# Head norm and output gate moved from the batch and the projection to the quarter that reads them, in a fused RWKV and cross-attention kernel

## What is computed

```python
xa = _ln(x, ln1_w, ln1_b)
sx = jnp.concatenate([state[:, 1:2] - xa[:, :1], xa[:, :-1] - xa[:, 1:]], axis=1)
xxx = jnp.tanh((xa + sx * maa_x) @ maa_w1).reshape(b, l, 5, DM)
xxx = jnp.einsum('blfd,fde->blfe', xxx, maa_w2)
xm = xa[:, :, None] + sx[:, :, None] * (maa_stack + xxx)      # five mixes
w = jnp.exp(-jnp.exp(time_decay + jnp.tanh(xw @ td_w1) @ td_w2))
r, k, v = xr @ Wr.T, xk @ Wk.T, xv @ Wv.T
g = jax.nn.silu(xg @ Wg.T)
def step(s, rkvw):                                            # 128 steps, per head
    a = k_t[..., :, None] * v_t[..., None, :]
    out = jnp.einsum('bhi,bhij->bhj', r_t, u * a + s)
    s = a + w_t[..., :, None] * s
    return (s, out)
og = ((og - m) / jnp.sqrt(va + 1e-05)).reshape(b, l, e) * gn_w + gn_b   # norm by head
x1 = x + og * g @ Wo.T
...                                                           # second layernorm and shift: xk2, xr2
y = x1 + sigmoid(xr2 @ Wfr.T) * (square(relu(xk2 @ Wfk.T)) @ Wfv.T)
# then per batch: instance norms, 1x1 convolutions, softmax attention of y over ctx, 1x1 convolution, + y
```

## Time and profile before

| | us |
|---|---|
| median of three runs | 1023.35 (1020.78 to 1023.88) |
| the profiled execution | 1016.36 |
| its span from first to last instruction | 1014.6 |
| PE busy | 896.1 (88%) |
| DVE busy | 691.5 (68%) |
| POOL busy | 536.5 (53%) |
| ACT busy | 396.5 (39%) |
| mean granted TensorE clock | 0.936 of 2.4 GHz |

### The profile page before, as it was taken

How to read it: one execution, slowest core, us unless ns; L and a number is a source line. 1 busy time by engine, 2 the same in 40 slices (tenths; PEclk the granted TensorE clock), 3 DMA queues, 4 the chain that set the end, 5 groups by cost and what they waited for, 6 DMA issues and landing times.

```text
span 1014.6 us, 10745 instructions
## 1 busy us (share of the span) xinstructions
PE 896.1 (88%) x3588; PEld 398.5 (39%) x3588; DVE 691.5 (68%) x907; ACT 396.5 (39%) x819; POOL 536.5 (53%) x573
## 2 busy tenths in 40 slices
PE   1679978799786899688998999899998999979998
PEld 1233433343322343243343444344443454444454
DVE  6234499789988687888887698988998224442342
ACT  2013412333212241133223254565355554465395
POOL 2000388669987749648886778889682101000010
PEclk9687997899977899698999999999999999999999
DMA  7351679969689877878979844779642022001001
GB/s 270 134 125 73 179 178 222 233 171 233 162 187 216 209 184 196 212 145 224 243 182 281 216 112 100 183 192 227 163 99 83 21 73 83 21 4 39 21 0 42
DMA packets 100089, 150.69 MB, mean 149 GB/s; under 512 B 22850, under 2 KB 64066, under 8 KB 91842
## 3 DMA queue, kind: packets, MB, share of 16 engines
q1 hardware_dynamic: 73410, 129.03, 50.4%
q10 hardware_dynamic: 26624, 20.98, 8.5%
HBM read 115.38 MB, written 33.55 MB: 147 GB/s over the span
## 4 chain that ended last, share of the span: by engine, by line
PE 59%; DVE 14%; POOL 12%; issue 6%; ACT 5%; ACTq 2%; DMA 2%; SPq 0%; POOLq 0%; DVEq 0%
PE PS L1318 38%; PE PS L1381 4%; PE PS L1543 4%; POOL VB L704 4%; PE PS L1440 3%; PE PS L1520 2%; DVE PS L1033 2%; PE PS L1325 2%; POOL VB L699 2%; DVE VB L1150 2%; DVE M L1030 2%; DVE VB L1030 2%; POOL VB L695 2%; DVE M L1033 2%; PE PS L1454 1%
## 5 line engine op out<-in xcount | busy, mean ns | idle before, releaser
L1318 PE MATMUL PS<-M,W 128*128 128x512 f32 x672 | 329.8, 634 | 23.7 <-DVE M L1033 12.3
L1318 PEld LDWEIGHTS PS<-M,W 128*128 128x128 f32 x672 | 128.7, 202 | 198.2 <-issue 167.5
L704 POOL TENSOR_TENSOR VB<-VB 128x1024 f32<-128x1024 f32 x64 | 151.4, 2366 | 58.9 <-ACT VB L849 56.2
L1150 DVE TENSOR_TENSOR_SCAN VB<-PS,VB 128x512 f32<-128x512 f32 x128 | 149.1, 1206 | 25.9 <-POOL VB L704 17.3
L587 POOL TENSOR_SCALAR NM<-MV 128x2 f32<-128x2 f32 (+1 forms) x24 | 6.2, 258 | 283.7 <-DVE MV L1278 183.0
L1030 DVE TENSOR_TENSOR VB<-VB,PS 128x2048 f32<-128x2048 f32 x64 | 145.9, 2280 | 1.5
L695 POOL TENSOR_TENSOR VB<-KR,VB 128x1008 f32<-128x1008 f32 x64 | 129.7, 2026 | 17.5 <-DMA VB<-scr_vs 17.5
L699 POOL TENSOR_TENSOR VB<-WG,VB 128x1008 f32<-128x1008 f32 x64 | 129.3, 2020 | 0.0
L1033 DVE SCALAR_TENSOR_TENSOR PS<-PS,VEC,SX 128x512 f32<-128x512 f32 x80 | 60.2, 752 | 87.7 <-PE PS L1381 72.4
L1318 PE MATMUL PS<-W,M 128*128 128x512 f32 x224 | 105.1, 595 | 0.0
L1296 DVE TENSOR_REDUCE SM<-PS 128x1 f32<-128x512 f32 x64 | 44.0, 688 | 58.9 <-PE PS L1543 58.4
(11 more groups left out here) (167 smaller groups left out, 1280.5 us busy)
## 6 DMA issues: line engine op xcount, KB each, us to landing
VB<-scr_vs SPq DMA_DIRECT2D x64, 1024.0 KB, 7.9
W<-in_w SPq DMA_DIRECT2D x8, 1024.0 KB, 9.8
X<-in_x SPq DMA_DIRECT2D x4, 1024.0 KB, 8.2
scr_vs<-STG ACTq DMA_DIRECT2D x64, 64.0 KB, 5.7
scr_v<-STG ACTq DMA_DIRECT2D x16, 256.0 KB, 6.9
scr_w<-STG ACTq DMA_DIRECT2D x16, 256.0 KB, 8.3
scr_k<-STG ACTq DMA_DIRECT2D x16, 256.0 KB, 2.7
KR<-scr_k SPq DMA_DIRECT2D x16, 256.0 KB, 8.1
```

What stands on the lines that cost most here:

```text
L704: po.tensor_tensor(flat(bv[:, 0]), flat(bv[:, 0]), flat(bv[:, 1]), ALU.add).then_inc(g_kv, 1)
L1150: sc = dv.tensor_tensor_scan(s_, PS[:, 5, :], b_, 0.0, ALU.mult, ALU.add)
L1318: mm = pe.matmul(o, l, r, start=i == 0, stop=i == 3)
```

## The change

1. **Norm by quarter.** After OT is assembled it is stored at once: `end` loses ACT's square and copy, PE's two small products, POOL's Newton steps and DVE's last multiplication. In c, `norm_gate` (ACT) squares the loaded quarter, 4 x 512 columns; PE takes the variance of a quarter with 16 matmuls of 128 columns; POOL runs Newton on 128 columns (`stream_n`) and writes a masked 128x512 operand; PE spreads it with one matmul of 512 columns; DVE (`normed`) does twelve `scalar_tensor_tensor`: times gn_w and the root, (tanh + 1) times g, plus gn_b times that.
2. **Gate by quarter.** ACT stores g/2 (`ACT.Copy`, scale 0.5); tanh is taken in c. `gate`, `affine` and `gated` are gone, and DVE has no p stream.
3. **Banks.** For the first three mixes of quarter 0 chunks 2 and 3 go to banks 6 and 7, the others stay in 0 and 1.
4. **Pairs.** For f < 4 DVE adds xa for two chunks in one instruction of 1024 elements, and `v_mad` counts pairs.
5. **v's copies** are issued by SP (`store_v`), in the same written order as the loads of the scan; a slot of STG freed by v also waits for its four rearranged copies.
6. **Waits by chunk.** `four_mm` and `four_turns` wait before each matmul for its own chunk (for the projections, its own pair).
7. **GpSimd's sum** covers columns 1 to 63 only (1008 elements), so L849 is gone, and DVE's scan waits for ACT's state column in place of POOL.
8. The five written orders are new. POOL's constants are a stream of their own.

```diff
+for _t in TAKES_A:
+    if _t[0] == "mix":
+        BANK_A[_t] = _t[3] % 2 + (6 if _t[1] == 0 and _t[2] < 3 and _t[3] // 2 else 0)
...
+            def store_v(q, m):
+                w.wait_ge(a_cp, 12 * q + m + 1)
+                ss = SLOT_STG["v", q, m]
+                for g in range(4):
+                    rows = STG[32 * g:32 * g + 32, ss, :].rearrange("h (s n) -> h s n", n=N2)
+                    sp.dma_start(vs_late[q, m, g], rows).then_inc(d_vs[m], 16)
+                    yield
+                sp.dma_start(dr["v"][q, m], STG[:, ss, :]).then_inc(d_st_["v"][m], 16)
+                yield
...
                     w.wait_ge(g_kv, 3 * k + 2)
-                    w.wait_ge(a_s0, 2 * k + 2)
-                    po.tensor_tensor(flat(bv[:, 0]), flat(bv[:, 0]), flat(bv[:, 1]), ALU.add).then_inc(g_kv, 1)
+                    po.tensor_tensor(vo, vo, ve, ALU.add).then_inc(g_kv, 1)
...
+            def stream_n():
+                for q in range(NQ):
+                    w.wait_ge(a_gv, q + 1)
+                    yield from newton(GR[:], GV[:], GT[:], g_gn, 14 * q)
+                    ...
+                    po.tensor_tensor(btv(SQ(q)[:, 0, :]), GR[:].unsqueeze(1).to_broadcast([P, 4, L]),
+                                     MASK[:].unsqueeze(2).to_broadcast([P, 4, L]), ALU.mult).then_inc(g_gn, 1)
...
-                    ac.activation(STG[:, ss, :], PS[:, n, :], ACT.Tanh, scale=0.5).then_inc(a_gt, 1)
+                    ac.activation(STG[:, ss, :], PS[:, n, :], ACT.Copy, scale=0.5).then_inc(a_gt, 1)
...
-                        yield from store(NAMES[0], q, m)
...
-                    ac.activation(VB[:, k % NB, 1, :, 0], S0[:, k, :], ACT.Copy, scale=0.0).then_inc(a_s0, 1)
-                    yield
...
+            def norm_gate(q):
+                for m in range(4):
+                    w.wait_ge(d_og, 16 * (q + 1))
+                    w.wait_ge(p_fr, 4 * q)
+                    ac.activation(SQ(q)[:, m, :], OG(q)[:, m, :], ACT.Square).then_inc(a_sq, 1)
+                    yield
+                ...
+                ac.activation(GV[:], PS[:, n, 0:L], ACT.Identity, bias=EB[:]).then_inc(a_gv, 1)
+                yield
+                for m in range(4):
+                    w.wait_ge(p_gn, 2 * q + 2)
+                    w.wait_ge(d_gl, 16 * (q + 1))
+                    ac.activation(SQ(q)[:, m, :], XN[:, m, :], ACT.Tanh).then_inc(a_gate, 1)
+                    yield
...
+                        two = slice(ec - 1, ec + 1)
+                        tt(M[:, two].rearrange("p c (b t) -> p c b t", t=L),
+                           PS[:, n - 1:n + 1].rearrange("p c (b t) -> p c b t", t=L), EXT[:, two, :, 1:L + 1],
+                           ALU.add).then_inc(v_mad, 1)
...
                     w.wait_ge(g_kv, 3 * (k + 1))
+                    w.wait_ge(a_s0, k + 1)
...
-                    tt(OT[:], OT[:], PS[:, 7, 3 * L:4 * L].unsqueeze(1).to_broadcast([P, C4, L]), ALU.mult).then_inc(v_ot, 1)
+            def normed(q):
+                O, G, n = OG(q), SQ(q), BANK_C[q, "rstd"]
+                for m in range(4):
+                    w.wait_ge(p_gn, 2 * q + 2)
+                    stt(O[:, m, :], O[:, m, :], vec(V_GNW + m), PS[:, n, :], ALU.mult, ALU.mult).then_inc(v_scl, 1)
+                for m in range(4):
+                    w.wait_ge(a_gate, 4 * q + m + 1)
+                    stt(G[:, m, :], G[:, m, :], 1.0, XN[:, m, :], ALU.add, ALU.mult).then_inc(v_gate, 1)
+                    w.wait_ge(v_gate, 4 * q + m + 1)
+                    stt(O[:, m, :], O[:, m, :], vec(V_GNB + m), G[:, m, :], ALU.add, ALU.mult).then_inc(v_y, 1)
...
                 for i, (l, r) in enumerate(pairs):
+                    if ready:
+                        ready[0].wait_ge(ready[1], ready[2] + i // (ready[3] if len(ready) > 3 else 1) + 1)
                     mm = pe.matmul(o, l, r, start=i == 0, stop=i == 3)
...
+                    for c in range(C4):
+                        for b in range(QB):
+                            mm = pe.matmul(PS[H * b:H * b + H, n, 0:L], SAME[:, 0], SQ(q)[:, c, b * L:(b + 1) * L],
+                                           start=c == 0, stop=c == C4 - 1)
+                    mm.then_inc(p_gn, 1)
...
+                    pe.matmul(PS[:, n, :], SAME[:].rearrange("p g h -> p (g h)"), SQ(q)[:, 0, :], start=True,
+                              stop=True).then_inc(p_gn, 1)
```

More of the change, by code:

```diff
@@ L326, in rwkv_attention_kernel @@
         p_tra, p_low, p_mix, p_td1, p_prj = [sem("p_" + n) for n in ("tra", "low", "mix", "td1", "prj")]
[L327 removed]
+        p_scan, p_wol, p_end, p_gn = [sem("p_" + n) for n in ("scan", "wol", "end", "gn")]
         p_wo, p_trc, p_fk, p_fr, p_fv = [sem("p_" + n) for n in ("wo", "trc", "fk", "fr", "fv")]
[L330 to L331 removed]
+        v_sta, v_aga, v_sub, v_m1, v_mix, v_mad = [
+            sem("v_" + n) for n in ("sta", "aga", "sub", "m1", "mix", "mad")]
         v_sc, v_pr, v_kr2, v_ot, v_wm, v_hd = [
             sem("v_" + n) for n in ("sc", "pr", "kr2", "ot", "wm", "hd")]
+        v_gate, v_scl = sem("v_gate"), sem("v_scl")
         v_y, v_xa, v_stc, v_agc, v_subc, v_kr, v_rk, v_x2 = [
@@ L782, in store @@
                 w.wait_ge(a_cp, 12 * q + 4 * "vkr".index(n) + m + 1)
-                if n == "v":
-                    for g in range(4):
-                        rows = STG[32 * g:32 * g + 32, SLOT_STG[n, q, m], :].rearrange("h (s n) -> h s n", n=N2)
-                        ac.dma_start(vs_late[q, m, g], rows).then_inc(d_vs[m], 16)
-                        yield
                 ac.dma_start(dr[n][q, m], src).then_inc(d_st_[n][m], 16)
@@ L1134, in stream_a @@
                         yield from first_mix(q + 1)
-            def stream_p():
-                for q in range(NQ):
-                    for m in range(4):
-                        gate(q, m)
-                        yield
             def stream_scan():
@@ L1306, in stream_l @@
                     yield
-            weave(ORDER_DVE, {"a": stream_a(), "p": stream_p(), "scan": stream_scan(), "end": stream_end(), "c": stream_c(),
+            weave(ORDER_DVE, {"a": stream_a(), "scan": stream_scan(), "end": stream_end(), "c": stream_c(),
                               **{n: stream_l(i) for i, n in enumerate(LANES)}})
@@ L1330, in turn_a @@
             def turn_a(q, ec):
-                w.wait_ge(a_xn, 4 * (q + 1))
                 w.wait_ge(g_id, 2)
                 n = banks.take(w, BANK_A["tr", q, ec], a_ext, 4 * q + ec + 1)
-                yield from four_turns(n, [XN[:, b, ec * P:(ec + 1) * P] for b in range(QB)], p_tra)
+                yield from four_turns(n, [XN[:, b, ec * P:(ec + 1) * P] for b in range(QB)], p_tra, (w, a_xn, 4 * q))
             def low_a(q, part):
-                w.wait_ge(v_m1, 4 * (q + 1))
                 w.wait_ge(d_lr, 32)
@@ L1340, in low_a @@
                 if part == 0:
-                    yield from four_mm(PS[:, n, :], [(W1[:, ec, 0:P], M1[:, ec, :]) for ec in range(C4)], p_low)
+                    yield from four_mm(PS[:, n, :], [(W1[:, ec, 0:P], M1[:, ec, :]) for ec in range(C4)], p_low,
+                                       (w, v_m1, 4 * q))
                 else:
@@ L1372, in mix @@
                         for ec in (2 * j, 2 * j + 1):
-                            banks.take(w, BANK_A["mix", q, f, ec], v_mad, 20 * q + 16 + 2 * j + 2)
+                            banks.take(w, BANK_A["mix", q, f, ec], v_mad, 10 * q + 8 + j + 1)
                         rows_mm((0, 1), DM, (W2[:, 4 + 2 * j], W2[:, 5 + 2 * j]), XXB, p_mix, False)
@@ L1376, in mix @@
                         w.wait_ge(d_xr, 64 * (q + 1))
-                        ns = [banks.take(w, BANK_A["mix", q, f, ec], v_mad, 20 * q + 4 * f + ec + 1)
+                        ns = [banks.take(w, BANK_A["mix", q, f, ec], v_mad, 10 * q + 2 * f + j + 1)
                               for ec in (2 * j, 2 * j + 1)]
@@ L1393, in project @@
                 n = banks.take(w, BANK_A["prj", q, f, m], *freed)
-                yield from four_mm(PS[:, n, :], [(W[:, wi, ec, m * P:(m + 1) * P], M[:, ec, :]) for ec in range(C4)], p_prj)
+                yield from four_mm(PS[:, n, :], [(W[:, wi, ec, m * P:(m + 1) * P], M[:, ec, :]) for ec in range(C4)], p_prj,
+                                   (w, v_mad, 10 * q + 2 * f, 2))
             def hidden(q):
-                w.wait_ge(v_mad, 20 * q + 8)
+                w.wait_ge(v_mad, 10 * q + 4)
                 w.wait_ge(d_wl, 64)
```

194 lines of the change are left out of this document (86 added, 108 removed), and 170 rows, old and new, of tables (ORDER_ACT, ORDER_DVE, ORDER_PE, ORDER_POOL).

## The result

The changed kernel takes 1068.02 us (median of 4 runs, 1062.47 to 1069.73), beside 1023.62 us of the kernel before on the same chip (1020.78 to 1024.17). The ratio is 1.043, with a 95% interval of 1.0387 to 1.0474: **slower by 4.3%**, where 981 us was forecast. The profiled execution has a span of 1068.0 us and a mean clock of 0.918; before it was 1014.6 and 0.936.

The account below looks back on a forecast made before the run. Engine hand-overs bound the first half, PE's work the second. Start -15, quarters 1 to 3 -25, 475 to 775 us -3, PE's tail work -2.3, norm path +3: -42 from 1023.35 gives 981 us, range 948 to 1018.

Parts of the forecast that it names:

- VectorE's term of nought: VectorE apart from the paired adds: 33 us of operations gone, 35 us new, nothing in total; about 20 less before 475 us.
- What bounds the kernel: Whole kernel: hand-overs between engines bound the first half, PE's work the second; nearly no idle time or lost clock behind 475 us.
- Start: Before the scans: 5 us from waits and banks, 5.4 from v's copies, 5 from both; 15 us in all, bounds 8 and 22.
- SP keeps up: At the start, SP issues v's copies in 3.3 us a chunk against the 3.5 us in which PE makes it.
- Pairs: VectorE's adds in four quarters: 64 become 32 of 1024 elements, 44.2 to 40.7 us, 3.5 us saved.
- GpSimd: its time: GpSimd's Newton steps shrink by 40 us, its sums by 2, and 56.2 us of waiting go; busy time near 494 us.
- Quarters 1 to 3, -25: 125 to 475 us: VectorE's relief lets idle time and lost clock close, 25 us gained, bounds 0 and 48.
- 475 to 775 us, -3: Between 475 and 775 us: of 12 us of PE's idle time, 3 may go.
- Last scan's sum near 780 us: Sign that the forecast is right: the last scan's sum, behind 664 us of PE's work in the new order.
- Tail and norm, +3 (17 with the cover gone): Tail: the path from loaded quarter to Wo grows to 21 us; 3 us shows, 17 without other work covering it.
- Slower, by SP's queue: Rival: in quarters 1 to 3 v's stores queue behind waiting loads, 26 us late three times; 1060 us, chance 0.11.
- The written orders miss: Rival: in the whole kernel, gains are met by new waits of the same size; 1023 us, chance 0.05.

Follow-up runs that it names:

- run 5: Changed kernel with three waits added on GpSimd (within scan step 26, before steps 40 and 44) until VectorE has finished named instructions; 1039.88 us, ratio 1.0176.
- run 7: The kernel of run 5 with VectorE's twelve norm operations cut to four products, without gn_w, gn_b, root and sigmoid; 1034.68 us, ratio 1.0117.
- run 8: Kernel before, old orders, with v's stores on SyncE alone and the loads of the state and x ahead of quarter 0's stores; 1036.57 us, ratio 1.012.
- run 9: The old-order kernel with four small parts and three GpSimd waits, plus quarter 0's v stores alone issued by SyncE; 997.42 us, ratio 0.981.
- 6: Kernel before, old orders, with four small parts (banks, pairs, waits by chunk, GpSimd's sum) and GpSimd waits at steps 13, 26, 52; 1014.59 us, ratio 0.9927.
- run 4: Kernel before, old orders, with four small parts only: banks 6 and 7, pairs, waits by chunk, GpSimd's sum without the state column; 1024.64 us, ratio 1.002.
- runs 1: Changed kernel with v's stores issued by ScalarE again, right behind each chunk's copy; 1074.24 us, ratio 1.0519.
- 10: The kernel of run 5 with v's stores issued by ScalarE again, right behind each chunk's copy; 1050.99 us, ratio 1.0338.
- runs 3: Kernel before, old orders, with v's stores on SyncE alone, quarter 0's ahead of the loads of the state and a small constant; 1055.01 us, ratio 1.0299.

## Why the prediction was wrong, point by point

The forecast of 981 us was missed by 87: a gain of 42 didn't come, and a loss of 44 came. The step that failed is VectorE's term of nought, below: waits that keep its instructions clear of GpSimd's return 28 of the 44 (run 5). Of the rest some 5 are the norm's (run 7), and the cause of the last 11 stays open.

**What bounds the kernel: half right.** The first half is held by hand-overs. But "nearly nothing behind 475 us" was read as safe. Before's second half was closed in its own orders; with the new orders and parts it opened: 50 of the 52.5 us that the ledger lost lie there.

**Start: mechanism right, but SyncE did not keep up.** Forecast 15 us, measured 4.9. The tanh of the decay does come at 58.9 us ("before 62"). But "SP keeps up" failed. The chain of after from the last v chunks on (start, duration, what):

```profile
50.88 0.61 SPq L463
51.53 2.08 SPq L483
53.66 0.55 SPq L463
...
62.76 7.62 DMA scr_v<-STG
70.45 0.70 ACT STG L833
...
73.04 11.67 PE PS L1331 x22
```

Five issues of 0.6 us a chunk left no room, the state's load took 2.08 us among them, and the last store's 7.62 us to land stands between ScalarE and its next slot. So the wait for the landing took the place of the issues on the chain; the prediction counted such a wait only in quarter 1. k's projection starts at 73.0 us ("before 72"). The size of the terms was not what failed. The prediction had 5 us for waits and banks, 5.4 for the issues and 5 for both together. Where the stores run undisturbed they gave 8.5 us (run 8) and 11.2 (run 9 against 6), the other parts 10 (run 4), and all together 21.4 at step 0 (run 9 against before), near the bound of 22.

The Trainium skill (DMA: Bandwidth & Descriptors, Issuing engines are not separate DMA queues) calls the issuing engine's time usually small; by it the 5.4 us would have been near nought. Here the measurement decides otherwise: moving these issues alone was worth 8.5 and 11.2 us of the ledger at step 0.

**Pairs: right.** 3.5 us forecast; 32 additions take 39.1 us (1223 ns each) where 64 took 44.2, which saves 5.1.

**VectorE otherwise "nothing in total": the step that failed.** Its busy time rose by 24.7 us, 24 of them in M<-SX. Each duration was taken from a row's mean as if it belonged to the instruction. The mean of M<-SX, 868 ns in before, already held stretched ones. This row of before's timeline stands beside GpSimd's first product of a step, which starts at 126.91 us:

```profile
126.92 2.53 DVE L1033 SCALAR_TENSOR_TENSOR M<-SX,VEC,EXT 128x512 f32<-128x512 f32 x1
```

The prediction freed GpSimd of 96 us of Newton steps and waiting and named no work that this would be moved onto. Yet such small steps and waits were what VectorE's mixes stood beside: 43 of the 48 M<-SX had no work of GpSimd on VB beside them in before, 29 in after. The three waits of run 5 put such gaps back and return 28 us (2.5% by the ratios).

The Trainium skill (SBUF — State Buffer, Who interferes with whom) has the rule that speaks against this change and that was not weighed: a VectorE instruction with two SBUF inputs contends with a GpSimd instruction that reads SBUF, and one of them blocks until the other is done. The traces agree: 2.32 us each beside GpSimd's 2.44, 0.67 without it, and 743 ns each with an operand in PSUM.

**GpSimd: its time right, its worth not.** Forecast 494 us busy, measured 501.7, and 493.5 once collisions are held off (run 5). The sum over 1008 elements, taken as 2.33, measured 2.39 in after and 2.34 in run 9. The 56.2 us of waiting for ScalarE became 115.3 for loads. In the chain that ended last GpSimd's share fell and VectorE's rose, from before:

```profile
PE 59%; DVE 14%; POOL 12%; issue 6%; ACT 5%; ACTq 2%; DMA 2%; SPq 0%; POOLq 0%; DVEq 0%
```

to after:

```profile
PE 59%; DVE 20%; issue 5%; ACT 4%; POOL 4%; DMA 4%; SPq 3%; ACTq 0%; DVEq 0%; POOLq 0%
```

So GpSimd left most of the chain, VectorE took a part of its place, and the time did not fall. VectorE's wait for the state column doesn't show in after, as forecast; its wait for ScalarE's copy of w does (above).

**Quarters 1 to 3, -25: wrong.** Idle time in the three windows rose from 56.6 to 64.2 us, and the clock was 0.86 to 0.87, not above 0.92. The term rested on VectorE's relief by 20 us; in these windows its busy time fell from 292 to 286 us and not to 272. Half of the best case was a choice without a row behind it.

**475 to 775 us, -3: wrong by some 50 in the ledger.** Last scan's sum near 780 us was the test, and it came at 878.

**Tail and norm, +3 (17 with the cover gone): about right in size.** Run 7 puts the chain at 5 to 6 us, all of it ahead of step 63 and not in the tail, where the prediction had it; PE's wait for the root ahead of the last quarter's Wo is 2.4 us.

**The rivals.** "Slower, by SP's queue" had a time near the result (1060) by another mechanism, so that nearness is luck. Its chance went to a cause that the runs refuse as the main one for the new orders (runs 1 and 10) and find at one place in the old ones (runs 3 and 8: some 20 us, where it had 26). "The written orders miss" was nearest in kind, but was priced as gains met by equal waits, with no mechanism that could go beyond nought.

## What to carry to other kernels

Before freeing or moving work of GpSimd, list VectorE's instructions with both operands in SBUF on the path, and look beside which GpSimd instructions they stand. A mean that lies far above that of the same form elsewhere can be a collision that is already there; the instructions one by one show it. If a group must be quick, a wait on GpSimd for it can be worth more than GpSimd's time: one wait gave 14 to 17 us here. And take a change of many parts apart: its four small parts and quarter 0's stores, with three waits on GpSimd, make the kernel 1.9% faster, where the whole made it 4.3% slower.
